# A Mamba-style block with FP4 FFN on one core: the scan's batches without a loop, and another order of work in the opening

## The reference, cut to what matters

```python
x = u                                   # (8 batches, 512 tokens, 512 features), float32
# layer part 1, the state-space block
z, xBC, dt = split(x @ in_proj_w.T)     # 1024 z, 1024 x + 128 B + 128 C, 64 dt columns
xBC = silu(causal_conv4(xBC) + conv_b)
dt = softplus(dt + dt_bias)
y = chunked_scan(x, dt, -exp(A_log), B, C) + x * D      # chunks of 64 tokens, 64 heads of 16
yg = y * silu(z)
x = layernorm(x + rmsnorm(yg) * norm_weight @ out_proj_w.T)
# layer part 2
gate, up = split(x @ fp4_decoded(gate_up).T)
x = layernorm(x + rmsnorm((silu(gate) * up) @ fp4_decoded(down).T))
```

## Time and profile before

| what | us |
|---|---|
| median of 3 runs | 1739.78 (1738.59 to 1742.42) |
| the profiled execution, its own time | 1741.6 |
| its span, first to last instruction | 1739.8 |
| busy: PE / DVE / ACT / POOL | 1566.7 / 1306.4 / 902.9 / 1118.7 |
| mean granted TensorE clock | 0.975 |

### The profile page before, as it was taken

The page is one execution under the profiler, slowest core; times in us unless marked ns, Lnnn a source line. Parts: engine busy times, 40 slices in busy tenths (PEclk is TensorE's granted clock), DMA queues, the critical chain, the costliest instruction groups (busy, mean ns, idle before and its releaser), DMA issues.

```text
span 1739.8 us, 43037 instructions
## 1 busy us (share of the span) xinstructions
PE 1566.7 (90%) x14272; PEld 767.3 (44%) x14272; DVE 1306.4 (75%) x2016; ACT 902.9 (52%) x1575; POOL 1118.7 (64%) x1087
## 2 busy tenths in 40 slices
PE   2699999989989898898998997878999999999998
PEld 1244445445445444444444443443444444444443
DVE  6939868868868877877976976657777777777774
ACT  2454354364454445445445444327766666666662
POOL 0038728838937837846855864967777776777773
PEclk9889999999999999999999999889999999999999
DMA  6121151142142134124015017420111110101011
GB/s 234 44 61 31 29 117 53 24 107 63 23 96 73 28 65 105 26 58 116 20 48 127 20 47 186 116 40 31 49 50 37 49 62 24 61 29 56 31 31 61
DMA packets 214777, 110.01 MB, mean 63 GB/s; under 512 B 133876, under 2 KB 185776, under 8 KB 214576
## 3 DMA queue, kind: packets, MB, share of 16 engines
q1 hardware_dynamic: 214576, 107.37, 23.0%
HBM read 80.57 MB, written 26.76 MB: 62 GB/s over the span
## 4 chain that ended last, share of the span: by engine, by line
PE 50%; issue 15%; POOL 15%; DVE 12%; ACT 3%; DMA 2%; SPq 1%; POOLq 1%; DVEq 0%; ACTq 0%
PE ps_in L779 9%; PE ps_in L939 8%; PE ps_yo L954 6%; PE ps_yd L954 6%; POOL xend L1677 5%; PE ps_in L801 5%; PE ps_s L939 4%; PE ps_t L939 4%; POOL y L1697 3%; DVE pre L1282 2%; POOL y L1691 2%; POOL zg L1706 2%; DVE mix L1370 2%; POOL sq L1714 1%; POOL sq L1715 1%
## 5 line engine op out<-in xcount | busy, mean ns | idle before, releaser
L1677 POOL TENSOR_TENSOR xend<-xpad,decay 128x256 f32<-128x256 f32 x256 | 225.5, 901 | 85.8 <-PE ps_yo L878 47.6
L1087 ACT ACTIVATE decay<-ps_d 128x512 f32<-128x512 f32 x256 | 150.5, 593 | 246.1 <-PE ps_d L841 136.6
L779 PE MATMUL ps_in<-u_hi,w_hi 128*128 128x512 f16 x576 | 221.5, 385 | 33.3 <-DVE pre L1282 16.1
L801 PE MATMUL ps_in<-w_out,zg 128*128 128x512 f32 x512 | 233.5, 610 | 9.2 <-DVE pre L1282 8.8
L779 PE MATMUL ps_in<-u_lo,w_hi 128*128 128x512 f16 x576 | 220.6, 383 | 0.0
L779 PE MATMUL ps_in<-u_hi,w_lo 128*128 128x512 f16 x576 | 220.4, 383 | 0.0
L1775 POOL TENSOR_TENSOR gate_sum<-gate_sum,gate_part 128x512 f32<-128x512 f32 x88 | 142.3, 1617 | 103.5 <-DVE gate_part L1598 103.2
L1370 DVE TENSOR_TENSOR mix<-decay,gb 128x1024 f32<-128x1024 f32 x128 | 182.3, 1424 | 30.9 <-ACT decay L1087 16.0
L1282 DVE SCALAR_TENSOR_TENSOR pre<-ps_in,cws,pre 128x511 f32<-128x511 f32 (+2 forms) x240 | 179.1, 746 | 19.0 <-ACT pre L1027 13.2
L801 PEld LDWEIGHTS ps_in<-w_out,zg 128*128 128x128 f32 x512 | 96.8, 194 | 143.2 <-issue 123.9
L939 PE MATMUL ps_in<-xt_hi,gu_w 128*128 128x512 f16 x352 | 133.9, 380 | 5.7 <-DVE gate_sum L1598 2.5
(11 more groups left out here) (187 smaller groups left out, 3682.2 us busy)
## 6 DMA issues: line engine op xcount, KB each, us to landing
ebc<-e_dram SPq DMA_DIRECT2D x256, 64.0 KB, 2.6
u<-u_t SPq DMA_DIRECT2D x9, 1024.0 KB, 5.3
res<-u_tok SPq DMA_DIRECT2D x32, 256.0 KB, 3.7
x_dram<-res SPq DMA_DIRECT2D x32, 256.0 KB, 2.1
xa<-x_dram SPq DMA_DIRECT2D x8, 1024.0 KB, 5.6
xr<-x_dram SPq DMA_DIRECT2D x32, 256.0 KB, 2.6
out<-xr SPq DMA_DIRECT2D x32, 256.0 KB, 2.1
fw_words<-gu_words SPq DMA_DIRECT2D x32, 176.0 KB, 4.0
```

The source lines that it names most:

```text
L779: last = mm(ps_in[bk][:, :], w[:, k, col:col + P], u[:, k, :], start=(k == 0 and j == 0), stop=(k == KT - 1 and j == 2))
L801: last = mm(ps_in[bk][:, :], zg[:, k, tt * P:(tt + 1) * P], w_out[:, k, :], start=(k == 0), stop=(k == CT - 1))
L1087: ac(decay[:, n % NG, :, :].rearrange("p a b -> p (a b)"), ps_d[n % 2][:, :], ACT.Exp).then_inc(e_done, 1)
L1677: g_.tensor_tensor(xend[:, pairs, :], xpad[:, c % 2, pairs, :], decay[:, g, :, CH - 1:CH].broadcast_to([P, CT, 2 * HD]), ALU.mult).then_in ...
```

## The change

Two things. The six looped bodies are written out one behind the other on all five engines, with constants for every target and address. And the opening is ordered anew: z0, z1 and z2 are projected among x4 to x7; the exponents and transposes `a1`, `a2`, `e0` to `e2` stand behind z7; the low halves of blocks 2, 3 and 4 are made on GpSimd, as a plain subtraction, for which ScalarE first scales the float32 weights in place (`weights_scaled`, one more activation per k tile); and VectorE's order of taps and dt steps is another.

```diff
--- before.py
+++ after.py
@@ -73,10 +73,11 @@
 
 
 HEAD = ["a0", "z1", "z2", "e0", "a1", "e1", "z3", "a2", "e2", "z4", "z5", "z6", "z7"]
-TAIL = {"pro": ["x7", "z0"] + HEAD, "body": ["x6", "x7", "z0", "o3", "q3"] + HEAD, "last": ["o3", "q3"]}
+PRO_ORDER = ["dt", "B", "C", "x0", "x1", "x2", "x3", "x4", "z0", "x5", "z1", "x6", "z2"]
+TAIL = {"pro": ["x7", "z3", "z4", "a0", "z5", "z6", "z7", "e0", "a1", "e1", "a2", "e2"], "body": ["x6", "x7", "z0", "o3", "q3"] + HEAD, "last": ["o3", "q3"]}
 AUX_ORDER = (0, 2, 1)
 NA = len(AUX_ORDER)
-PRO_USES = [(0, "dt"), (0, "B"), (0, "C")] + [(0, f"x{i}") for i in range(CT - 1)]
+PRO_USES = [(0, name) for name in PRO_ORDER]
 BODY_USES = [(4, "dt"), (5, "B"), (7, "C"), (9, "x0"), (11, "x1"), (12, "o0"), (13, "q0"), (17, "x2"), (19, "x3"),
              (20, "o1"), (21, "q1"), (25, "x4"), (27, "x5"), (28, "o2"), (29, "q2")]
 LAST_USES = [(12, "o0"), (13, "q0"), (20, "o1"), (21, "q1"), (28, "o2"), (29, "q2")]
@@ -365,6 +366,7 @@
         w_out_done = sem("w_out_done")
         w_hi_done = sem("w_hi_done")
         w_lo_done = sem("w_lo_done")
+        w_scaled = sem("w_scaled")
         u_in = sem("u_in")
         res_in = [sem(f"res_in{tt}") for tt in range(TT)]
         rq_in = [sem("rq_in0"), sem("rq_in1")]
@@ -711,7 +713,7 @@
             store_parts(0)
             load_head(0)
             body(Stage("body", 0))
-            with sp.Fori(1, nb - 1) as i:
+            for i in range(1, nb - 1):
                 body(Stage("body", i))
             body(Stage("last", nb - 1))
 
@@ -924,7 +926,7 @@
             tail(pro)
             pe.wait_ge(w_out_done, 1)
             body(Stage("body", 0))
-            with pe.Fori(1, nb - 1) as i:
+            for i in range(1, nb - 1):
                 body(Stage("body", i))
             body(Stage("last", nb - 1))
 
@@ -1137,10 +1139,16 @@
                     elif name[0] == "z":
                         take_z(st, name)
 
-            def weights_hi(block):
+            def weights_hi(block, tiles=range(KT)):
                 col, n = W_BLOCKS[block]
-                for k in range(KT):
+                for k in tiles:
                     ac(w_hi[:, k, col:col + n], w_src(k, col, n), ACT.Identity, scale=w_in_scale).then_inc(w_hi_done, 1)
+
+            def weights_scaled(block, tiles):
+                col, n = W_BLOCKS[block]
+                weights_hi(block, tiles)
+                for k in tiles:
+                    ac(w_src(k, col, n), w_src(k, col, n), ACT.Identity, scale=w_in_scale).then_inc(w_scaled, 1)
 
             act.wait_ge(small_in, N_SMALL)
 
@@ -1154,23 +1162,26 @@
             exp_dt(0)
             take_conv(pro, "B")
             take_conv(pro, "C")
-            weights_hi(2)
-            for i in range(CT - 1):
-                if i == 5:
+            weights_scaled(2, range(2))
+            for name in PRO_ORDER[3:]:
+                if name == "x5":
 
                     act.wait_ge(w_lo_done, KT * 3)
-                take_conv(pro, f"x{i}")
-                if i == 2:
+                if name[0] == "z":
+                    take_z(pro, name)
+                    continue
+                take_conv(pro, name)
+                i = int(name[1])
+                if i < 4:
+                    weights_scaled(*((2, range(2, KT)), (3, range(2)), (3, range(2, KT)), (4, range(KT)))[i])
+                if i == 4:
                     ln_dt(0)
-                if i == 4:
                     exp_cs(0)
-                if i in (3, 5):
-                    weights_hi(i // 2 + 2)
             act.wait_ge(const_in, N_CONST)
             act.wait_ge(pro_pool, 1)
             tail(pro)
             body(Stage("body", 0))
-            with act.Fori(1, nb - 1) as i:
+            for i in range(1, nb - 1):
                 body(Stage("body", i))
             body(Stage("last", nb - 1))
 
@@ -1566,23 +1577,23 @@
             taps(pro, "C")
             dve.wait_ge(const_in, N_CONST)
             v.tensor_scalar(to_top[:, :], shift[:, :], 28, None, ALU.bitwise_xor)
-            dt_second(0, 1)
-            weights_lo(2)
-            for i in range(CT):
-                if i < 3:
-                    dt_second(0, 2 + i)
-                if i == 3:
-                    dt_third(0)
+            taps(pro, "x0")
+            for i in range(1, 4):
                 taps(pro, f"x{i}")
-                if i in (3, 5):
-                    weights_lo(i // 2 + 2)
+                dt_second(0, i)
+            dt_second(0, 4)
+            taps(pro, "x4")
+            taps(pro, "x5")
+            dt_third(0)
+            taps(pro, "x6")
+            taps(pro, "x7")
             measure_u(1)
             dve.wait_ge(w_out_in, 16)
             for k in range(CT):
                 last = v.tensor_scalar(w_out[:, k, :], w_out[:, k, :], normw[:, k:k + 1], None, ALU.mult)
             last.then_inc(w_out_done, 1)
             body(Stage("body", 0))
-            with dve.Fori(1, nb - 1) as i:
+            for i in range(1, nb - 1):
                 body(Stage("body", i))
             body(Stage("last", nb - 1))
 
@@ -1762,9 +1773,17 @@
             reduce_u(0)
             pool.wait_ge(pro_dve, MAXES_READY)
             g_.partition_all_reduce(maxes_all[:, :], maxes[:, :], P, RMAX).then_inc(pro_pool, 1)
+            pool.wait_ge(w_lo_done, 2 * KT)
+            for block in range(2, len(W_BLOCKS)):
+                col, n = W_BLOCKS[block]
+                for k in range(KT):
+                    pool.wait_ge(w_hi_done, KT * block + k + 1)
+                    pool.wait_ge(w_scaled, KT * (block - 2) + k + 1)
+                    g_.tensor_tensor(w_lo[:, k, col:col + n], w_src(k, col, n), w_hi[:, k, col:col + n], ALU.subtract)\
+                        .then_inc(w_lo_done, 1)
             reduce_u(1)
             body(Stage("body", 0))
-            with pool.Fori(1, nb - 1) as i:
+            for i in range(1, nb - 1):
                 body(Stage("body", i))
             body(Stage("last", nb - 1))
 
```

## The result

The changed kernel takes 1729.09 us (median of 4 runs, 1728.04 to 1729.69), against 1739.9 for the kernel before on the same chip: a ratio of 0.9936, 95% interval 0.9919 to 0.9952. That is 10.8 us faster. Forecast were 1732.4, a range of 1726 to 1739, and 0.76 for faster by over 0.2%. The direction and the range held; the gain was larger than the 7.4 us of the sum. Two executions, one of the kernel before (1880 us) and one of e12 (2315 us), ran at a mean granted clock of 0.84 and 0.66 and are left out of every median and ratio here.

What follows compares the result with a forecast made beforehand. VectorE was taken to bound the opening up to 87.37 us, then TensorE. Opening -4.3 and loop -3.1 (registers -3.9, crossings +0.8) gave -7.4 us: 1734.2 from the profiled execution, 1732.4 against the median, range 1726 to 1739.

Steps and rivals of the forecast that it cites:

- What bounded the opening: Opening: VectorE sets the pace, through low halves of weights (2.65 us per block) and dt steps ahead of bank-freeing taps.
- Opening, the sum: Start to batch 1's dt tile: -13.1 work off VectorE, +2 slower dt steps, +3.5 clock, +3.3 exponents, together -4.3 us.
- Contention: Opening: GpSimd's subtractions slow VectorE's dt steps between x0 and x4; 2 us taken, bounds 0 and 10.6.
- upper bound of 10.6: Opening: 7.9 us of dt parts all slowed as L1308's steps are in a body, 2.12 to 4.96 us.
- clock term: Opening: TensorE pauses between z0 and x5, so about one tile runs at the lower clock; 3.5 us, bounds 0 and 9.
- Exponents behind z7: First crossing, z7 to next dt tile: ScalarE's exponent work, hidden before, now stands unhidden and delays the dt tile 3.3 us.
- Registers: Looped bodies, dt tile to z7: constants instead of registers save 0.65 us for each of six, -3.9 us.
- Crossings: Between bodies, z7 to next dt tile: jump stall hidden by ScalarE, straight crossings set to the mean 10.84; +0.8 us.
- Rival B: Between bodies: each of five removed jumps back gives its full 2.97 us, -14.9; total 1716.7 us; chance 0.05.
- Rival E: Opening: TensorE stays at its lower clock from z0 to z7, 2.7 us per tile; 1745.1 to 1750.5 us; chance 0.07.
- C: Opening gives nothing: dt steps suffer 3.3 us more, one more tile at the lower clock; 1736.7 us; chance 0.20.
- D: Opening gives nearly all, -9.8 us: no contention, no tile at the lower clock; 1726.9 us; chance 0.18.

Runs made afterwards that it cites:

- e12: Changed kernel with the opening's old tile order, low halves still on GpSimd and VectorE's new order kept; 1730.24 us, ratio 0.9953.
- e9: Changed kernel with low halves of blocks 2, 3 and 4 back on VectorE, without ScalarE's scaling in place, new tile order kept; 1731.94 us.
- e10: Changed kernel with each of GpSimd's twelve subtractions preceded by the same one into an unused tile; 1736.21 us, ratio 0.9975.
- e8: The changed kernel as it is, run and profiled once more; 1728.06 us, ratio 0.9930.
- e11: e6 plus extra matmuls into an unused bank in the opening, 16 ahead of x5 and 3 each ahead of x6 and x7; 1723.87 us.
- e6: Changed kernel with ten added 512-column matmuls in each body's slot 1, their result overwritten; 1726.97 us, ratio 0.9927.
- e7: Changed kernel with the opening's exponents and transposes put back ahead of z7, among z5, z6 and z7; 1729.11 us, ratio 0.9928.
- e2: Kernel before with the six looped bodies written out on all five engines, old opening kept; 1733.85 us, ratio 0.9955.
- e4: Changed kernel with the hardware loop kept on VectorE alone, other engines straight; 1735.71 us, ratio 0.9966.
- e1: Changed kernel with the hardware loop of bodies 1 to 6 put back on all five engines, new opening kept; 1737.32 us, ratio 0.9974.
- e3: Changed kernel with the hardware loop kept on TensorE alone, other engines straight; 1737.23 us, ratio 0.9977.

## Why the prediction was right

**The number.** The range held, the sum did not: against -7.4 stand -11.9 us of span, and most of what is missing is in one term, the crossings, whose sign was wrong.

**What bounded the opening.** VectorE, as said, up to x4: shown by e9, where its three blocks come back and batch 1's dt tile moves by 6.1 us.

**Opening, the sum.** Forecast -4.3, measured 4.92 less (121.34 to 116.42), in openings that spread over 2 to 3 us. Its terms: z7 at 102.6 forecast, 103.30 measured; z7 to the dt tile about 14.5 forecast, 13.12 measured, so that two misses of 0.7 and 1.4 with opposite signs meet in the sum. Contention was set at 2 us and was 14.4 - 11.2 = 3.3: four dt steps of about 0.42 took 1.15 to 1.27. The upper bound of 10.6 was reached by e10 (22.0 - 11.2 = 10.8), so the bound from L1308 was about right. What the Trainium skill says of the shared port (SBUF — State Buffer, "Who interferes with whom") held here for two SBUF inputs and for the taps with one; e10 adds that `tensor_scalar` of 128x256 float32 with one SBUF input goes from 0.29 to 1.13 us, which the same section allows for its two-port modes. The clock term, 3.5 us, was too large: x5 ran partly at the lower level (0.63 granted from 69.81 to 73.30), and z7 came 1.1 us earlier in e8, where it did not, and 1.4 earlier in e11, where the pauses are filled, than in e6. The forecast's reading that TensorE had done nothing for 6.3 us before its clock fell was off as well: the mean of 0.87 from 48.30 to 54.60 says that it fell within that pause.

```profile
69.81:73.30 3.49, 3.49 (x11) 1.37 (x12) 0.00 (x0) 0.00 (x0) 0.00 (x0) 0.63 0.00 0
```

**Exponents behind z7**, 3.3 us: 3.6 by e7. Against the kernel before, the first crossing grew by 1.96 only: its 11.16 us (clock 0.69) were long for this code, which took 9.52 in e2 (0.82), and the forecast put its 3.3 on top of them. What the forecast did not see is that the order of tiles as a whole is then worth next to nothing (0.4 us in e12), since it only moves the same work from one side of z7 to the other.

**Registers**, -3.9: measured -3.66, and it is VectorE's queue (e4). The close agreement is partly made: forecast and measurement both count the body of 126.27 us with its wait for a DMA. e1, which has no such body, sums to 752.20, 2.8 more than the changed kernel, about 0.46 us for each body.

**Crossings**, +0.8: this step failed, and its sign was wrong. The forecast said that the stall behind a jump is hidden by ScalarE and that straight crossings are as long as the mean of all seven. The five crossings behind a jump became 2.1 us shorter, not 0.8 longer, and crossing 1, for which the forecast had nothing, became 1.9 shorter. Both premises came from too few rows. The first jump was the only one whose TensorE timeline was read the earlier trace rows, and its matmul started at 3.78 us after z7, still under ScalarE's cover; in three of the other four it did not, and ScalarE waited 0.24, 0.61 and 0.87 us, 1.7 in all. And the two straight crossings of the kernel before, 11.16 and 11.27, were both at a low clock (0.69 and 0.71), which straight crossings have only at times: of the changed kernel's six, two. The 1.9 us of crossing 1 are such a difference between two executions and no merit of the change. Rival B priced the other extreme, the full 2.97 us for each of five jumps: 14.9 us. The rule of the Trainium skill that it goes by (Runtime: NRT & Kernel Launch, "Instruction fetch mechanics": a taken branch whose target is not among the code already fetched stalls the engine until it is) agrees with TensorE's stalls here. But their price in the kernel before is about 0.4 us per jump (2.1 for five), since ScalarE covers the rest; in e3 ScalarE's waits alone are 0.8 per jump.

**Rival E** is out: z0 to z7 did not run at the lower level (the mean clock up to z7 was 0.97). **C** and **D** missed the opening on either side.

## What to carry to other kernels

A stall of one engine behind a loop's jump costs only what sticks out from under the engine that sets the pace; so read every iteration, not the first, and compare the start of the stalled instruction with the moment at which the pacing engine wants it. Where two halves of a reordering sit on either side of the event that you count to, measure at the next event that both must pass: the new tile order looked like 4 us at z7 and was 0.4 at the dt tile. Low-clock time in a recurring pause of TensorE can be bought back with matmuls whose result is overwritten, if they fit into the pause: the six crossings gained 3 to 4 us here, which the time of the whole program did not yet show beyond its noise. And before a difference between two profiles is put down to a change, look at the same kernel profiled twice, and at a piece that the change does not touch: single crossings of the changed kernel moved by up to 1.9 us from one profile to the next, and so did crossing 1 between before and after.

## What the runs showed of the hardware that was not expected

- Single crossings of the same code take 9.4, 10.1 or 11.25 us from one execution to the next (the changed kernel and e8), while the sum of six stays within 1.2 us (60.70 and 59.49). TensorE had paused for about 2.5 us in the crossing.
- Ten added matmuls of 512 columns (2.33 us) in each crossing made the six crossings shorter (56.39 against 60.70 and 59.49), by keeping the granted clock at 1.00.
- Behind a jump TensorE stalls in two places: 1.17 us at the jump, and 2.97 us after one more exponent matmul and four transposes (e3, 648.66 to 652.64). In the kernel before, the second stall was 2.7 to 3.7 us. VectorE, too, stands still for 2.7 to 3.1 us behind its jump (e4), and the bodies with such a stall at their end are no longer than the one without.
- GpSimd's subtractions on SBUF made dependent VectorE steps of 0.42 us last 1.15 to 1.26, close to one whole GpSimd instruction (1.16), not a share of it.

Not tried: the loop on ScalarE, GpSimd or SP alone, and VectorE's new order of taps without the rest. With the loop on VectorE alone six crossings sum to 62.80, above the 59.5 to 61.9 of the other kernels without a jump on TensorE; ScalarE never waits there for the second exponent matmul, so that this, too, goes with the clock (0.70 to 0.73 in three), but no second profile shows how often it happens.
